# A two-layer transformer kernel: the steps of the first attention regrouped by TensorE setting, and its partial sums in two buffers

## Time and profile before

| what | value |
|---|---|
| times of three runs | 1947.33, 1948.58, 1945.76 us |
| median | 1947.33 us |
| span of the profiled execution, first to last instruction | 1942.0 us |
| PE busy in the span | 1723.3 us (89%) |
| DVE busy | 1364.9 us (70%) |
| ACT busy | 1229.6 us (63%) |
| POOL busy | 507.7 us (26%) |
| mean granted TensorE clock | 0.943 |

### The profile page before, as it was taken

The page is one execution under the profiler, slowest core; times in us unless marked ns, Lnnn a source line. Parts: engine busy times, 40 slices in busy tenths (PEclk is TensorE's granted clock), DMA queues, the critical chain, the costliest instruction groups (busy, mean ns, idle before and its releaser), DMA issues. The chain is left out here.

```text
span 1942.0 us, 35641 instructions
## 1 busy us (share of the span) xinstructions
PE 1723.3 (89%) x12164; PEld 1029.1 (53%) x12164; DVE 1364.9 (70%) x2932; ACT 1229.6 (63%) x1752; POOL 507.7 (26%) x813
## 2 busy tenths in 40 slices
PE   5999999999999999993966499999999999669993
PEld 3556655666566556652963134343334343439992
DVE  6677677777777777774548598888888884245664
ACT  5888888878888888771655236666665667214443
POOL 1221121223121411131441112222512424133441
PEclk9999999999999999996988679999999999789996
DMA  5111111101111101103223513231311310312225
GB/s 180 50 39 39 39 36 39 37 25 49 39 36 39 47 26 39 36 24 133 62 79 131 183 32 55 39 61 32 83 32 42 73 32 14 124 33 57 60 61 146
DMA packets 101189, 115.66 MB, mean 60 GB/s; under 512 B 15467, under 2 KB 75212, under 8 KB 100397
## 3 DMA queue, kind: packets, MB, share of 16 engines
q1 hardware_dynamic: 94454, 100.22, 18.7%
q0 software_dynamic: 6592, 13.56, 2.1%
HBM read 78.86 MB, written 34.41 MB: 58 GB/s over the span
## 5 line engine op out<-in xcount | busy, mean ns | idle before, releaser
L1724 ACT ACTIVATE a_p<-a_score 128x1024 f32<-128x1024 f32 (+3 forms) x384 | 302.5, 810 | 218.6 <-PE a_score L1746 212.2
L1852 DVE TENSOR_REDUCE a_mx<-a_misc 128x1 f32<-128x512 f32 (+3 forms) x768 | 380.3, 549 | 45.7 <-PE a_misc L1779 33.5
L306 ACT ACTIVATE a_p<-a_score 128x1024 f32<-128x1024 f32 (+3 forms) x384 | 292.6, 816 | 36.3 <-PE a_score L343 35.2
L248 POOL TENSOR_SCALAR_AFFINE_SELECT a_p<-a_p 128x256 f32<-128x256 f32 x256 | 125.8, 521 | 640.9 <-ACT a_p L324 640.9
L1776 PE MATMUL a_misc<-a_k,a_q 72*128 72x512 bf16 (+3 forms) x768 | 251.7, 348 | 30.4 <-DVE a_out L1970 22.0
L324 ACT ACTIVATE a_p<-a_p 128x2560 f32<-128x2560 f32 (+1 forms) x128 | 273.9, 2140 | 1.1
L362 PE MATMUL a_out<-a_p,a_v 128*64 128x512 f32 (+3 forms) x1536 | 269.9, 493 | 0.0
L343 PE MATMUL a_score<-a_q,a_k 64*128 64x512 f32 (+3 forms) x2304 | 266.7, 361 | 3.1 <-ACT a_p L306 1.5
L1746 PE MATMUL a_score<-a_q,a_k 128*128 128x512 bf16 (+3 forms) x768 | 234.1, 330 | 6.8 <-ACT a_p L1724 6.6
L343 PEld LDWEIGHTS a_score<-a_q,a_k 64*128 64x128 f32 x2304 | 185.6, 186 | 85.0 <-issue 41.2
L522 DVE TENSOR_TENSOR a_part<-a_part,a_p 128x1024 f32<-128x1024 f32 (+3 forms) x256 | 223.6, 873 | 7.7 <-ACT a_p L324 0.9
(11 more groups left out here) (301 smaller groups left out, 2613.8 us busy)
## 6 DMA issues: line engine op xcount, KB each, us to landing
a_xt<-xt SPq DMA_DIRECT2D x31, 512.0 KB, 3.4
a_q<-qk_parts SPq DMA_DIRECT2D x144, 64.0 KB
a_k<-qk_parts SPq DMA_DIRECT2D x144, 64.0 KB
e_xs<-f_x_rows SPq DMA_DIRECT2D x110, 64.5 KB, 1.8
qk_parts<-p_part SPq DMA_DIRECT2D x24, 256.0 KB, 6.4
xt<-a_p SPq DMA_DIRECT2D x9, 512.0 KB, 3.6
a_w<-in_l_attn_w SPq DMA_DIRECT2D x32, 128.0 KB, 3.1
values<-xt_all SPq DMA_DIRECT2D x4, 1024.0 KB, 7.3
```

The source lines that it names most:

```text
L248: last = nc.gpsimd.affine_select(out=blk, in_=blk, compare_op=ALU.is_ge, fill=0.0, base=0, pattern=[[0, 2], [1, P]], channel_multiplier=-1)
L306: nc.scalar.activation(chunk_of(prob[p], c), score_ps[:, c % 2, :, 0:width], ACT.Tanh, scale=scale / clamp).then_inc(tanh_done, 1)
L1724: nc.scalar.activation(prob[s % RING][:, :, 0:width], score_ps[:, s % 2, :, 0:width], ACT.Exp, scale=scale).then_inc(exp_done, 1)
L1852: nc.vector.tensor_reduce(m[c][:, h, t:t + 1], misc[:, bank, 0:keys], AX_X, ALU.max).then_inc(free, 1)
```

```diff
-        part = k.sb("a0_part", [P, 2, SEQ])
+        part = [k.sb(f"a0_part{i}", [P, 2, SEQ]) for i in range(2)]
+        sums = k.sb("a0_sums", [P, HALF])
...
-        QK_JOBS, V_JOBS = {0: "k0", 2: "q0", 3: "k1", 5: "q1"}, {4: 0, 7: 1}
+        QK_JOBS = {2: ("k0", "k1"), 6: ("q0", "q1")}
...
+        def act_sum(act, m):
+            if not exists(m):
+                return
+            act.wait_ge(summed, m + 1)
+            ge(act, recip, m)
+            nc.scalar.copy(sums[:], misc[:, 0, :]).then_inc(sum_out, 1)
+
...
-            act_out(act, u - 2, 1)
...
+                if i == 8:
+                    if exists(u):
+                        act_v(act, u, p, 0)
+                        act_v(act, u, p, 1)
+                    act_out(act, u - 1, 1)
...
+                if i == 4:
+                    act_sum(act, u - 1)
+
+
+        def matmul_by_cols(out, lhs, rhs):
+
+            for c in range(2):
+                cols = slice(c * DH, (c + 1) * DH)
+                mm = nc.tensor.matmul(out[cols, :], lhs[:, cols], rhs, start=True, stop=True)
+            return mm
...
+            if name == "q0":
+                pe.wait_ge(evac["k0"], n + 1)
+                ge(pe, sum_out, n - 1)
+            if name == "q1":
+                pe.wait_ge(evac["k1"], n + 1)
+                b, at = routed(n - 1)
+                if at in (2, 3):
+                    pe.wait_ge(routes.sems["xt"], 2 * b + at - 1)
+                elif at == 4:
+                    pe.wait_ge(routes.sems["logits"], b + 1)
+                elif at == 5:
+                    pe.wait_ge(routes.sems["counted"], b + 1)
...
-                mm = nc.tensor.matmul(misc[:, half, t * P:(t + 1) * P], xt[:, tile * P:(tile + 1) * P],
-                                      wv[p][:], start=True, stop=True)
+                mm = matmul_by_cols(misc[:, half, t * P:(t + 1) * P], xt[:, tile * P:(tile + 1) * P], wv[p][:])
...
-            if exists(m + 1):
-                pe.wait_ge(evac["v0"], m + 2)
+            if exists(m + 2):
+                pe.wait_ge(evac["k0"], m + 3)
...
         def dve_recip(dve, m):
-            dve.wait_ge(summed, m + 1)
+            dve.wait_ge(sum_out, m + 1)
             ge(dve, bcast[1], m)
-            nc.vector.reciprocal(rsum[:], misc[:, 0, :]).then_inc(recip, 1)
+            nc.vector.reciprocal(rsum[:], sums[:]).then_inc(recip, 1)
...
-            order = [("x", before, 0), ("norm", before, 1), ("split", nxt, "k0"), ("x", before, 1),
-                     ("split", nxt, "q0"), ("split", nxt, "k1"), ("adds", prev, 3), ("split", nxt, "q1"),
-                     ("recip", prev, None), ("r_high", prev, None), ("r_low", prev, None), ("adds", u, 0),
-                     ("adds", u, 1), ("norm", prev, 0), ("adds", u, 2)]
+            order = [("x", before, 0), ("x", before, 1), ("adds", prev, 3), ("split", nxt, "k0"), ("split", nxt, "k1"),
+                     ("adds", u, 0), ("recip", prev, None), ("r_high", prev, None), ("r_low", prev, None),
+                     ("split", nxt, "q0"), ("split", nxt, "q1"), ("adds", u, 1), ("adds", u, 2),
+                     ("norm", prev, 0), ("norm", prev, 1)]
```

More of the change, by code:

```diff
@@ L158, in attention0 @@
         added = sem("a0_added")
-        summed, recip, r_high, r_split = (sem(f"a0_{n}") for n in ("summed", "recip", "r_high", "r_split"))
+        summed, sum_out, recip, r_high, r_split = \
+            (sem(f"a0_{n}") for n in ("summed", "sum_out", "recip", "r_high", "r_split"))
         spread_made = sem("a0_spread_made")
@@ L307, in act_step @@
                                              scale=scale / clamp).then_inc(tanh_done, 1)
[L308 to L312, removed]
+                b, at = routed(u)
+                if i == 6 and at in (2, 3):
+                    routes.act_turned(act, b, at - 2, spare)
+                for name in QK_JOBS.get(i, ()):
+                    act_high(act, u + 1, 1 - p, name)
+                if i == 2 and at == 1:
+                    routes.act_deviation(act, b)
                 if i == 6:
                     act_out(act, u - 1, 0)
[L315 to L319, removed]
+                if i == 8:
[3 more added lines that the diff above has]
+                    act_out(act, u - 1, 1)
                 if i + 2 == GROUPS[g][1]:
@@ L392, in pe_v @@
                 ge(pe, x_added[half], n - 1)
+                if half == 0:
+                    ge(pe, sum_out, n)
             if half == 0:
@@ L415, in pe_sum @@
                     mm = nc.tensor.matmul(misc[row:row + 32, 0, :], ones[:, 0:32],
-                                          part[:, h, half * HALF:(half + 1) * HALF], start=True, stop=True)
+                                          part[p][:, h, half * HALF:(half + 1) * HALF], start=True, stop=True)
             mm.then_inc(summed, 1)
@@ L421, in pe_bcast @@
             pe.wait_ge(r_split, m + 1)
[L422 to L433, removed]
+            if exists(m + 1):
+                pe.wait_ge(evac[f"v{half}"], m + 2)
+            elif half == 1:
+                ge(pe, x_added[1], m)
             if isinstance(m, int) and m == 0 and half == 0:
@@ L445, in pe_wo @@
                 tile = half * (TILES // 2) + t
-                mm = nc.tensor.matmul(misc[:, half, t * P:(t + 1) * P], ot[:, tile * P:(tile + 1) * P],
-                                      wo[p][:], start=True, stop=True)
+                mm = matmul_by_cols(misc[:, half, t * P:(t + 1) * P], ot[:, tile * P:(tile + 1) * P], wo[p][:])
             mm.then_inc(wo_done[half], 1)
@@ L461, in pe_step @@
                     pe_scores(pe, u, p, both)
+                if i == 8 and exists(u):
+                    pe_v(pe, u, p, 0)
+                    pe_v(pe, u, p, 1)
                 if i % 4 == 0 and exists(prev):
@@ L464, in pe_step @@
                         pe_pv(pe, prev, 1 - p, c)
[L465 to L469, removed]
                 if i == 0 and exists(before):
+                    pe_wo(pe, before, p, 0)
                     pe_wo(pe, before, p, 1)
[L472 to L476, removed]
+                if i == 4 and exists(prev):
+                    pe_sum(pe, prev, 1 - p)
                 b, at = routed(u)
-                if i == 8 and at in (2, 3, 4, 5):
-                    pe.wait_ge(evac["v1"], u + 1)
+                if i == 6 and at in (2, 3, 4, 5):
+                    pe.wait_ge(evac["k1"], u + 2)
                     if at < 4:
@@ L485, in pe_step @@
                         routes.pe_rank(pe, b, spare)
-                if exists(prev):
-                    if i == 10:
-                        pe_wo(pe, prev, 1 - p, 0)
+                if exists(nxt):
+                    for name in QK_JOBS.get(i, ()):
+                        pe_qk(pe, nxt, 1 - p, name)
+                if i == 10 and exists(prev):
+                    pe_bcast(pe, prev, 0)
+                    pe_bcast(pe, prev, 1)
         def dve_split(dve, n, p, name):
@@ L584, in dve_step @@
                     dve_r_low(dve, m)
-                if (what, m, arg) == ("norm", prev, 0):
+                if (what, m) == ("r_low", prev):
                     if at == 4:
```

16 lines of the change are left out of this document (8 added, 8 removed).

## The result

The changed kernel takes 1979.73 us (median of four runs, 1968.97 to 1988.09) against 1946.55 for the kernel before, measured beside it: ratio 1.0182, 95% interval 1.0158 to 1.0206. It is slower, by 33 us; the forecast was 25 slower, range 1955 to 2005. The profiled execution took 1978.86, with a span of 1976.9 against 1942.0, 34.9 more.

A forecast was written before the change was run, and what follows sets the result against it. TensorE's list of work was taken to bound the first attention, and after the change a ring through the reciprocal. Ring 13, routed units 8 and clock 4 sum to +25 on 1947.3: 1972 us, range 1955 to 2005.

The forecast's parts named there:

- The ring sets the unit: First attention: values wait for q0's split behind the reciprocal; TensorE leg 14.1 plus ACT/DVE leg 12.3 makes 26.4 us a unit.
- TensorE's own 25.4: A unit of the first attention if nothing but the saved changes of setting moved: 25.4 us, from 25.97.
- The three changes: TensorE's changes of setting per unit fall from 16 to 13, at 0.2 us each: -0.6 us a unit.
- Pairs of half passes at 0.11: Values and outputs as two 64-column matmuls: a pair takes 0.11 us, as the single pass did, costing nothing.
- Reciprocal from SBUF, 3.35: VectorE's reciprocal of the sums, read from SBUF instead of PSUM: no gain, 3350 ns for 512 elements.
- Masks 1.50, VectorE free before the sums: POOL masks take 1.50 us, so DVE finishes its adds at 223.0, before the sums arrive at 223.4.
- Free edits: Second `part` buffer only loosens a wait; added copy uses free ACT time; DMAs and POOL's weight split keep their triggers.
- Routed units: Units that also route a batch: table loads +2.9 us, logits and rank about +1.9 each; +8 us in all.
- The clock: 4 us: TensorE's clock falls after stalls in three units, 1.4 us each; 4 us added.
- The rival with falls in half of the units: Clock falls in half of the units: 22 us in place of 4, 1990 us; many-falls rival's chance 0.17.
- a sign against me: Listed signs that would show the forecast wrong included half clock in plain units.
- The stages behind are shifted whole: Stages after the first attention keep their length and only move by its change; no separate gain or loss.

The follow-up runs named there:

- experiment 1: Changed kernel with VectorE's adds of group 1 and splits of q0 and q1 moved ahead of the reciprocal: 1909.15 us, ratio 0.9805.
- (3): Changed kernel with the reciprocal replaced by a VectorE copy, division left out: 1903.64 us, ratio 0.9796.
- experiment 4: Kernel before with the reciprocal replaced by a VectorE copy, division left out: 1930.97 us, ratio 0.9940.
- experiment 7: Changed kernel with one `part` buffer instead of two: 2044.81 us, ratio 1.0529.

## Why the prediction was right, step by step

- *The ring sets the unit.* Right. The stall stands ahead of the values, released by the split of q0; forecast 26.4 a unit, measured 26.49. Both legs were near: from the values at 201.24 to the second k cast at 215.26 is 14.0 (forecast 14.1), from there to the values at 227.72 12.5 (forecast 12.3, by the path over the copy of the sums; the path over the adds is the 0.2 longer one). Taking the split out from behind the reciprocal (experiment 1) or the reciprocal out of the ring (3) removes it whole.
- *TensorE's own 25.4.* Mis-sized: it is 24.70 (experiments 1, 3). The three changes are worth 0.54 to 0.65 (0.18 to 0.215 each), as the 0.6 of the sum. What was missed lay in the kernel before: 0.27 us of waiting that came from the reciprocal (experiment 4), and 0.33 in scores 10 and 11, where the second chunk waited for tanh. Those scores take 1.16 in the kernel before, by the rows below, and 0.83 in the kernel after (231.78 to 232.61), where values as well as chunks 8 to 11 stand ahead of them. So the stall is 1.7 to 1.8, the far end of the forecast. It did not matter to the forecast, since the ring and not TensorE set the unit; it matters to what a repair is worth.
- *Pairs of half passes at 0.11.* Right. The 62 ns a MATMUL of the Trainium skill ("TensorE: Matmul & The Clock Gate", section "Wait — 56ns, not 53.3ns?") hold where hardware decode is off; this step doesn't show them, since its 32 passes take 1.80 us, 56 ns each.
- *Reciprocal from SBUF, 3.35.* Right, 3.346.
- *Masks 1.50, VectorE free before the sums.* Masks right. But the adds behind them take 0.6 longer (2.85 for 2.27), because GpSimd's weight split now runs beside them, and the reciprocal starts 0.20 us after the end of the copy. "Keep their triggers within a unit and are due later" looked at when that work is due and not at what it now runs beside. Size: 0.2 us of the ring at most.
- *Free edits.* Not all free. The second `part` buffer "only loosens a wait", but the ring of the sum rests on adds that run early, and with one buffer the ring is 1.26 us longer (experiment 7).
- *Routed units.* Right where the clock doesn't fall. The unit of the rank runs from 408.59 to 437.05, 28.46, forecast 28.3. The one with table loads takes 30.99 (294.65 to 325.64) with a fall in it; less 1.7 that is 29.3, as forecast (26.4 + 2.9). With falls in nearly all such units they stand above the "28 to 29.5" that I gave.
- *The clock: 4 us.* The term that was too small, by its count and not its size: 1.7 a fall was measured for 1.4 assumed (2.3 for the three longer ones), but ten falls for three, some 19 us. The rival with falls in half of the units was nearer in this term. Falls in two plain units are what I had named as a sign against me.
- *The stages behind are shifted whole; the ends.* Not quite. Up to 208 us the kernel after is 1 us ahead (scores at 207.26 for 208.22), though its units are longer, because its first two are 3.6 us shorter; and behind the attention it wins back about 3: the broadcasts, last outputs and what follows.

The sum on the profiled spans: about 15 for the ring (29 x 0.53; forecast 13), some 19 for the clock (4), about -7 at both ends (0), and 7 to 8 for routing (8), which is what remains of the 34.9 measured. Sign and mechanism were right; that the 1972 came so near is in part luck, because two missed terms, the clock's +15 and the ends' -7, have opposite signs.

The timeline of TensorE before, for scores 10 and 11:

```profile
231.22 1.22 PE L343 MATMUL a_score<-a_q,a_k 64*128 64x256 f32 x12
232.38 0.73 PE L437 MATMUL a_misc<-a_rhl,a_spread 128*128 128x512 f32 x2
```

These twelve matmuls start over 1.16 us, with a gap of about 0.3 before the second chunk, released by ScalarE's tanh; of the same twelve after, none waits.

## What to carry to other kernels

When a regrouping saves time on the busiest engine, follow the data once round the ring that the new order closes, and look for the longest instruction on another engine that now stands between a producer and the step just moved. Here one line of VectorE's order turned 33 us lost into 34 won, with the gain of the regrouping (1.27 us a unit, half of it from the changes of setting) waiting behind a 3.35 us division. A wait on TensorE is paid twice where the clock falls behind it, so count the pauses too and not only their length; and put work that is in no hurry (table loads, weight splits) where its engine stands still already, and not beside an instruction on the ring.

## What the runs showed of the hardware

- **A pause of one length, two outcomes.** In the kernel after TensorE pauses 1.72 to 1.78 us in every plain unit. Over 200 to 300 us the granted clock stayed at 1.00 all the same; at 449.9 and 504.5, in two other plain units, it fell. A longer pause decides it no better. Ahead of the same projection, in the unit with the rank, TensorE paused 3.29 us in one batch with the clock at 1.00, and 3.30 in the next with a fall (0.77 over 640 to 655):

```profile
420.85 0.47 PE L415 MATMUL a_misc<-a_xh,a_wh 128*128 128x512 f32 x1 [3.29 <-DVE r_base L912]
415.00:430.00 15.00, 11.71 (x111) 8.01 (x111) 12.21 (x17) 11.31 (x16) 0.04 (x1) 1.00 0.18 54
```

  The four runs of this kernel differ by 1% (1968.97 to 1988.09) and line up with their mean clock: 0.940, 0.936, 0.935, 0.933 for 1968.97, 1978.86, 1980.6, 1988.09. What decides whether a given pause brings a fall stays open.
- **GpSimd and VectorE slow each other down.** The weight split (two inputs in SBUF) takes 0.74 alone and 1.52 beside VectorE's adds; the adds take 2.27 alone (experiment 7) and 2.85 beside it. The Trainium skill ("SBUF — State Buffer", section "SBUF: two separate sides") says that a shared pair of ports is held for a whole instruction by whichever starts first, a GpSimd instruction or, among others, a VectorE instruction with two inputs in SBUF. The rows agree: the first add, which starts 0.02 us ahead of the split, keeps its 0.95; the split takes 0.78 longer, and the two adds behind take 1.57 in place of 1.15. VectorE's copy, with one input, is slowed too (0.29 alone, 0.46 beside GpSimd's cast at 219.60). That it is the ports and nothing else is not shown by any run.
- **A change of setting costs 0.2 us.** 0.18 to 0.215, from lists of 15 and of 13 changes that differ otherwise only in full or half passes. The Trainium skill ("TensorEngine Tiling (Array Packing)", section "Key Properties") says that a change of mode drains TensorE. The rows here show a price for each change, not what TensorE does in that time.
